# Attention scores from high and low parts instead of full float32 products, with a new instruction order

## The chip, the cores and the metric

The kernel runs on one core of a Trainium2 chip. Its time is the device time of one execution in microseconds (us). The engines are TensorE (PE: matrix products; its weight loads are shown apart, as PEld), VectorE (DVE), ScalarE (ACT), GpSimd (POOL) and SyncE (SP, which issues the transfers).

## The reference, cut to what matters

Four layers run on 8 samples of 512 rows and 256 columns. Layer 0 is causal attention with 16 heads of 16 columns, layers 1 and 3 are gated attention (only the 256 rows with the highest gate take part), layer 2 is attention with 16 heads of 64 columns and a relative bias.

```python
def _L0_attn_a_ref(x, Wq, Wk, Wv, Wo):                 # causal
    Q, K, V = (proj(Wq), proj(Wk), proj(Wv))           # 16 heads, d_k = 16
    Q = _apply_rope(Q, cos, sin)
    K = _apply_rope(K, cos, sin)
    scores = jnp.einsum('bhnd,bhmd->bhnm', Q, K) / jnp.sqrt(jnp.asarray(d_k, x.dtype))
    scores = jnp.where(causal, scores, -jnp.inf)
    attn = jax.nn.softmax(scores, axis=-1)
    ...
def _L0_ffn_ref(token_inputs, Wg, Wq, Wk, Wv, Wo):     # gated
    gate = jax.nn.sigmoid((token_inputs @ Wg)[..., 0])
    _, idx = jax.lax.top_k(gate, C)                    # C = 256 of 512 rows
    attn_in = jnp.take_along_axis(token_inputs, idx[..., None], axis=1)
    ...                                                # q, k, v: 16 heads, dh = 16
    scores = jnp.einsum('bqhd,bkhd->bhqk', q, k) / jnp.sqrt(jnp.float32(dh))
    attn = jax.nn.softmax(scores, axis=-1)
    ...
x = L0_attn_a_x                                        # (8, 512, 256)
x = x + _L0_attn_a_ref(_layernorm(x, axis=-1), ...)
x = x + _L0_ffn_ref(_layernorm(x, axis=-1), ...)
x = x + _L0_attn_b_ref(_layernorm(x, axis=-1), ...)    # 16 heads of 64, relative bias
x = x + _L0_ffn_ref(_layernorm(x, axis=-1), ...)
```

## The kernel before

All eight samples stay on the one core. The work is cut into steps such as `c_q`, `c_p1` (causal layer), `f_p1` (gated layers) and `b_row`, `b_tr`, `b_val` (biased layer). Each step is one block of TensorE work with the work of the other engines on its result. `in_order` puts all steps of all samples into one list, by the written-out numbers in `PLACE` and a model with costs per step in `WORK`; each engine goes through this list and takes its own part of each step, in that order. While sample s is in its biased layer, the causal layer and the first gated layer of sample s+1 and the last gated layer of sample s-1 are laid between its steps. So from sample 1 on the same cycle of steps repeats. Samples 0 and 1 go through their causal and first gated layers ahead of any biased step, and the last gated layer of sample 7 is alone at the end. Where the model expects TensorE to wait by over 1 us, transposes without use are put in (line 1341), which fill the wait.

TensorE writes into 8 banks of PSUM, each 128 x 512 values, and each result is read out of its bank by DVE or ACT before the bank is used again.

A score of the causal and gated layers is a product over only 16 values. Four heads are computed side by side, in four groups of 32 rows of the array, into four banks. The 32 rows of a group hold two heads; for head e of the two, `Qz` and `K1` (`Qzf`, `K1f` in gated layers) hold the head's 16 rows, zeros in the other head's, and in one of these a row of ones and the negative row maximum. The scores are computed twice:

- The first time (`c_p1`, `f_p1`, lines 1379 and 1469) rows are queries, and DVE takes the maximum of each (lines 1176 and 1251) into `mcol`.
- `c_m` and `f_m` transpose the maxima on TensorE, and DVE adds them into the row of `Qz` (line 1184).
- The second time (`c_p2`, `f_p2`, lines 1399 and 1488) rows are keys and the maximum is subtracted within the product. ACT takes the exponential straight out of PSUM (lines 1057, 1068).
- `c_va`, `c_vb`, `f_va`, `f_vb` (lines 1413, 1500) multiply the values.

A `c_p1` or `c_p2` step has a number u: its key or query tiles are 128 and 256 columns wide (u = 0 in `c_p1`, u = 2 in `c_p2`), 384 (u = 1) or 512. There are four groups g of such steps in a layer, so 12 `c_p1` and 12 `c_p2` in a causal layer, 4 `f_p1` and 4 `f_p2` in a gated one (each 2 x 256 columns). All these products are full float32.

Ahead of the scores, a causal layer turns q and k (rope): DVE shuffles and multiplies (lines 1159, 1160), POOL multiplies and adds (lines 999, 1001), then `c_hq` (ACT, lines 1051 and 1052) and `c_hk` (DVE, 1165 and 1166) make the two heads' halves. In gated layers ACT (line 1062) and DVE (line 1240) make them straight out of PSUM. Products in the reduced format `F32R` are already there in `f_gather` and `f_y` (line 1322 with `of_hi`, `of_lo`), where one factor is 0 or 1 and the other is split into a high and a low part.

```python
for t, at_, w in parts:                                    # c_p1, from line 1379's block
    for h in range(4):
        last = te.matmul(o[h][:, at_:at_ + w], m.Qz[group(h), c, e, tile_of(t)],
                         m.K1[group(h), c, e, 0:w], start=True, stop=True)
```

## Time and profile before

| | |
|---|---|
| median of 3 runs | 2102.8 us (2101.93 to 2104.2) |
| profiled execution, its own time | 2105.06 us |
| its span | 2103.3 us |
| PE busy | 2029.9 us (97%) |
| DVE, ACT, POOL busy | 1467.4, 1110.2, 600.8 us |
| the chain that ended last | PE 85%, DVE 7%, ACT 6% |

The span is the stretch from the first to the last instruction on the engines in the profiled execution; 1.8 us of its own time lie around it. Busy times are sums of instructions. A busy PE counts the pipeline of a product too, so neighbouring products overlap in it; how fast PE goes is better read from when the next ones start.

### The profile page before, as it was taken

Reading aid. Unit: us, or ns where it says so; the run is one execution under the profiler, and the core shown is the slowest. Engines: PE = TensorE matmul, PEld = TensorE weight load, DVE = VectorE, ACT = ScalarE, POOL = GpSimd, SP = SyncE. Lnnn points to the kernel's source line nnn. Section 1 sums busy time; section 2 is a strip of 40 time slices with the busy share of each in tenths; the row PEclk is TensorE's granted clock in tenths of the full one; section 3 lists DMA queues with packets and bytes.
Section 4 is the critical chain, followed back from the end, with each engine's and each line's share of the span. In section 5 each row is a group of like instructions: output and inputs, shape, how many; then the busy total and the mean of one; then the engine's idle time right before and its main releaser. Section 6 shows DMA issues by size and latency. Waiting matters only on the chain.

```text
span 2103.3 us, 38722 instructions
## 1 busy us (share of the span) xinstructions
PE 2029.9 (97%) x14644; PEld 1243.3 (59%) x14644; DVE 1467.4 (70%) x4578; ACT 1110.2 (53%) x2497; POOL 600.8 (29%) x817
## 2 busy tenths in 40 slices
PE   7889999999999999999999999999999999999997
PEld 4456556655665555765566645666456654666565
DVE  8887654777757766678767687576875777866435
ACT  1444664746537474464734646365563656535642
POOL 4212132243222342233411423124231243212220
PEclk9999999999999999999999999999999999999998
DMA  3001121121111110111101111012100121111200
GB/s 143 2 1 41 43 76 58 50 81 34 44 41 57 57 44 26 48 67 48 42 21 58 58 47 44 18 59 71 46 31 27 51 73 49 44 34 51 76 3 11
DMA packets 29047, 98.56 MB, mean 47 GB/s; under 512 B 2880, under 2 KB 11200, under 8 KB 28736
## 3 DMA queue, kind: packets, MB, share of 16 engines
q1 hardware_dynamic: 28864, 96.09, 13.6%
q8 instruction: 118, 1.93, 0.4%
q14 instruction: 65, 0.53, 0.1%
HBM read 91.89 MB, written 4.19 MB: 46 GB/s over the span
## 4 chain that ended last, share of the span: by engine, by line
PE 85%; DVE 7%; ACT 6%; issue 1%; POOL 0%; DMA 0%; SPq 0%; DVEq 0%; ACTq 0%; POOLq 0%
PE ps L861 26%; PE ps L1532 11%; PE ps L1550 10%; PE ps L1322 9%; PE ps L1540 9%; PE ps L1379 4%; PE ps L1488 3%; PE ps L1399 3%; PE ps L1500 3%; PE ps L1469 3%; PE ps L1413 2%; ACT PTc L1057 2%; ACT PT L1097 2%; DVE ps L1176 2%; DVE mcol L1251 1%; ACT probs L1088 1%
## 5 line engine op out<-in xcount | busy, mean ns | idle before, releaser
L1015 POOL TENSOR_SCALAR probs<-probs,rtotal 128x512 f32<-128x512 f32 x512 | 344.9, 693 | 871.8 <-DVE rtotal L1277 871.3
L1088 ACT ACTIVATE probs<-probs,peak 128x512 f32<-128x512 f32 x512 | 365.0, 714 | 220.9 <-DVE peak L1273 220.9
L1268 DVE CUSTOM_DVE_ANT_0 probs<-ps,band 128x512 f32<-128x512 f32 x512 | 332.6, 687 | 107.8 <-PE ps L1532 106.4
L1097 ACT ACTIVATE PT<-ps 128x512 f32<-128x512 f32 x512 | 263.1, 619 | 78.1 <-PE ps L1540 77.9
L1176 DVE CUSTOM_DVE_ANT_0 ps<-ps,later 128x128 f32<-128x128 f32 (+3 forms) x512 | 233.3, 525 | 40.9 <-PE ps L1379 40.0
L1540 PEld LDWEIGHTS ps<-ident,probs 128*128 128x128 f32 x2048 | 223.3, 141 | 52.0 <-issue 43.3
L1532 PE MATMUL ps<-KT,QT 64*128 64x512 f32 x1024 | 252.4, 611 | 0.0
L1540 PE MATMUL ps<-ident,probs 128*128 128x128 f32 x2048 | 248.3, 275 | 0.1
L1550 PE MATMUL ps<-PT,Vb 128*64 128x512 f32 x1024 | 235.9, 600 | 0.1
L861 PE MATMUL ps<-xnT,wb 128*128 128x512 f32 x512 | 233.0, 598 | 1.3 <-ACT PT L1097 0.7
L1057 ACT ACTIVATE PTc<-ps 128x384 f32<-128x384 f32 (+1 forms) x384 | 167.7, 542 | 64.8 <-PE ps L1399 64.7
L1251 DVE TENSOR_REDUCE mcol<-ps 128x2 f32<-128x512 f32 x256 | 157.3, 683 | 14.8 <-PE ps L1469 14.0
L1068 ACT ACTIVATE PTf<-ps 128x512 f32<-128x512 f32 x256 | 131.7, 604 | 63.0 <-PE ps L1488 62.6
L861 PEld LDWEIGHTS ps<-xnT,wb 128*128 128x128 f32 x512 | 92.9, 190 | 102.0 <-issue 96.8
L1532 PEld LDWEIGHTS ps<-KT,QT 64*128 64x128 f32 x1024 | 94.5, 186 | 92.9 <-issue 67.9
L1550 PEld LDWEIGHTS ps<-PT,Vb 128*64 128x64 f32 x1024 | 67.1, 137 | 139.2 <-issue 121.8
L861 PEld LDWEIGHTS ps<-wb,xnT 128*128 128x128 f32 x1024 | 122.6, 192 | 26.5 <-issue 16.7
L1007 POOL TENSOR_SCALAR_AFFINE_SELECT PTc<-PTc 128x512 f32<-128x512 f32 x128 | 82.1, 654 | 178.0 <-ACT PTc L1057 177.3
L983 POOL TENSOR_TENSOR rstd<-veps,pow_half 128x2 f32<-128x2 f32 x64 | 47.0, 737 | 280.8 <-DVE veps L1118 280.8
L861 PE MATMUL ps<-wb,xnT 128*128 128x128 f32 x1024 | 125.7, 276 | 0.0
L1322 PE MATMUL ps<-wob,OTb 128*128 128x256 f32 x512 | 114.0, 380 | 0.8 <-DVE OTb L1279 0.8
L1379 PE MATMUL ps<-K,Qz 32*128 32x128 f32 (+3 forms) x1024 | 96.5, 471 | 14.8 <-ACT PTc L1057 4.9
(133 smaller groups left out, 2887.3 us busy)
## 6 DMA issues: line engine op xcount, KB each, us to landing
band<-in_band SPq DMA_DIRECT2D x64, 896.0 KB, 4.6
wb<-in_w_b SPq DMA_DIRECT2D x64, 384.0 KB, 3.0
x<-in_x SPq DMA_DIRECT2D x16, 256.0 KB, 2.9
out<-x SPq DMA_DIRECT2D x16, 256.0 KB, 2.2
wob<-in_wo_b SPq DMA_DIRECT2D x1, 1024.0 KB, 8.7
wqk<-in_wqk_a SPq DMA_DIRECT2D x1, 512.0 KB, 6.2
cos_t<-in_cos SPq DMA_DIRECT2D x1, 256.0 KB, 5.4
sin_t<-in_sin SPq DMA_DIRECT2D x1, 256.0 KB, 6.5
```

What stands on the lines that cost most here:

```text
L861: last = nc.tensor.matmul(o, w, r, start=(i == 0), stop=(i == len(pairs) - 1))
L1015: last = g.tensor_scalar(unit, unit, rtotal[:, r % 8, e:e + 1], 1.0, ALU.mult, ALU.mult)
L1057: a.activation(pt_c(m, q)[:, h], bank(now, name)[:, 0:w], ACT.Exp).then_inc(act_read, 1)
L1088: last = a.activation(unit, unit, ACT.Exp, bias=peak[:, r % 8, e:e + 1], accum_out=total[:, r % 8, e:e + 1])
L1097: a.activation(PT[:, k % 2, e, :, tile_of(q)], bank(now, name).rearrange("p (k n) -> p k n", k=NT), ACT.Copy).then_inc(act_read, 1)
L1176: last = v.tensor_tensor_reduce(out=scores, in0=scores, in1=later[:, NT * P - w:NT * P], scale=1.0, scalar=-3e38, op0=ALU.add, op1=ALU.max ...
L1268: v.tensor_tensor_reduce(out=probs[:, r % ROWS_HELD, e, :], in0=bank(now, name), in1=band[:, k % 2, e, lo:lo + T], scale=1.0, scalar=-3e38 ...
L1322: last = te.matmul(o[:, j * D:(j + 1) * D], w, r, start=(k == 0 and j == 0), stop=(k == count - 1 and j == 1))
L1379: last = te.matmul(o[h][:, at_:at_ + w], m.Qz[group(h), c, e, tile_of(t)], m.K1[group(h), c, e, 0:w], start=True, stop=True)
L1532: full(te.matmul(bank(now, name), QT2[half(e), k % 2, tile_of(q)], KT2[half(e), k % 2, :], start=True, stop=True), now, name)
L1540: last = te.transpose(bank(now, name)[:, tile_of(t)], probs[:, r % ROWS_HELD, e, tile_of(t)], ident[:])
L1550: last = te.matmul(o[half(e), :], Vb[:, k % 3, q, half(e)], PT[:, k % 2, e, q, :], start=(q == 0), stop=(q == NT - 1))
```

## The change

The scores of causal and gated layers are computed with F32R products of split factors, in the 32 rows of a group that were half zeros before. For one head, the 16 upper rows of `X` hold the high part of q and the 16 lower ones the low part. `HI` holds the high part of k twice, `LO` its low part twice. `X` with `LO` plus `X` with `HI` is then the whole product. A `c_p1` or `f_p1` step has two F32R products in place of each float32 one. `c_p2` and `f_p2` have three: the third takes the maxima, which are now split into high and low parts as well, from a tile `M`, with a small constant of minus ones (`sel`) as weights.

To make these parts, DVE shuffles q and k twice per block (`c_dq`, `c_dk`, `f_q`, `f_k`), so that a head's 16 rows stand in both halves. For q, POOL makes both parts (`c_xq`, `f_xq`: two multiplications by a column of minus ones and zeros, two additions). For k, ACT rounds to the high part (twice) and POOL subtracts it (twice; `c_hk`, `f_hk`). The maxima are split by DVE in two small operations (`c_hm`, `f_hm`), transposed on TensorE as before, and copied out of PSUM by ACT (`c_m`, `f_m`). The factor 1/4 of the scores moves into ACT's exponential, as its scale. Tiles lie elsewhere in memory, `Dq` shares its place with `PTc`, and `M1` with `HI`, from which new rules of order follow (`lent`). The two memsets on POOL in the causal layer of sample 1 are gone; DVE does them at the start. All numbers of `PLACE` are others, found anew with the new `WORK`.

```diff
-    "c_m": [("pe", 0.443), ("dve", 1.26)],
+    "c_hm": [("dve", 0.12), ("dve", 0.16)],
+    "c_m": [("pe", 0.443), ("act", 0.5)],
...
-    "f_q": [("pe", 1.727), ("act", 1.16)],
-    "f_k": [("pe", 1.727), ("dve", 1.44)],
+    "f_q": [("pe", 1.727), ("dve", 0.65), ("dve", 0.65)],
+    "f_xq": [("pool", 0.78), ("pool", 0.78), ("pool", 1.26), ("pool", 1.26)],
+    "f_k": [("pe", 1.727), ("dve", 0.65), ("dve", 0.65)],
+    "f_hk": [("act", 0.55), ("act", 0.55), ("pool", 1.26, 0), ("pool", 1.26, 1)],
...
-    "f_p1": [("pe", 0.963), ("dve", 0.598), ("dve", 0.598), ("dve", 0.598), ("dve", 0.598)],
-    "f_m": [("pe", 0.218), ("dve", 0.74)],
-    "f_p2": [("pe", 0.972), ("act", 0.477), ("act", 0.477), ("act", 0.477), ("act", 0.477)],
+    "f_p1": [("pe", 0.47), ("dve", 0.598), ("dve", 0.598), ("dve", 0.598), ("dve", 0.598)],
+    "f_hm": [("dve", 0.12), ("dve", 0.16)],
+    "f_m": [("pe", 0.218), ("act", 0.3)],
+    "f_p2": [("pe", 0.7), ("act", 0.477), ("act", 0.477), ("act", 0.477), ("act", 0.477)],
...
-    ("c_p1", 0): [("pe", 0.85), ("dve", 0.594), ("dve", 0.594), ("dve", 0.594), ("dve", 0.594)],
-    ("c_p1", 1): [("pe", 0.858), ("dve", 0.5), ("dve", 0.5), ("dve", 0.5), ("dve", 0.5)],
-    ("c_p1", 2): [("pe", 0.965), ("dve", 0.649), ("dve", 0.649), ("dve", 0.649), ("dve", 0.649)],
-    ("c_p2", 0): [("pe", 0.975), ("act", 0.477), ("act", 0.477), ("act", 0.477), ("act", 0.477), ("pool", 0.59)],
-    ("c_p2", 1): [("pe", 0.858), ("act", 0.37), ("act", 0.37), ("act", 0.37), ("act", 0.37), ("pool", 0.59)],
-    ("c_p2", 2): [("pe", 0.863), ("act", 0.37), ("act", 0.37), ("act", 0.37), ("act", 0.37), ("pool", 1.175)],
+    ("c_p1", 0): [("pe", 0.44), ("dve", 0.594), ("dve", 0.594), ("dve", 0.594), ("dve", 0.594)],
+    ("c_p1", 1): [("pe", 0.35), ("dve", 0.5), ("dve", 0.5), ("dve", 0.5), ("dve", 0.5)],
+    ("c_p1", 2): [("pe", 0.47), ("dve", 0.649), ("dve", 0.649), ("dve", 0.649), ("dve", 0.649)],
+    ("c_p2", 0): [("pe", 0.70), ("act", 0.477), ("act", 0.477), ("act", 0.477), ("act", 0.477), ("pool", 0.59)],
+    ("c_p2", 1): [("pe", 0.53), ("act", 0.37), ("act", 0.37), ("act", 0.37), ("act", 0.37), ("pool", 0.59)],
+    ("c_p2", 2): [("pe", 0.66), ("act", 0.37), ("act", 0.37), ("act", 0.37), ("act", 0.37), ("pool", 1.175)],
...
-    "c_hq": [("act", 0.96)],
-    "c_hk": [("dve2", 0.36), ("dve2", 0.36)],
+    "c_dq": [("dve", 0.65), ("dve", 0.65)],
+    "c_xq": [("pool", 0.78), ("pool", 0.78), ("pool", 1.26), ("pool", 1.26)],
+    "c_dk": [("dve", 0.65), ("dve", 0.65)],
+    "c_hk": [("act", 0.55), ("act", 0.55), ("pool", 1.26, 0), ("pool", 1.26, 1)],
...
+        out += [(c("q", i), [c("xt")], []), (c("k", i), [c("xt")], []), (c("dq", i), [c("q", i)], []),
+                (c("xq", i), [c("dq", i)], []), (c("dk", i), [c("k", i)], []),
+                (c("hk", i), [c("dk", i)], [])]
     out += [(c("v", i), [c("xt")], []) for i in range(2)]
+    lent = {0: [c("xq", 0), c("xq", 1)], 2: [c(w, i) for w in ("q", "k", "v") for i in range(2)]}
     for g in range(4):
         for u in range(3):
-            out.append((c("p1", g, u), [c("hq", g // 2), c("hk", g // 2)], [c("p1", g, u - 1)] if u else []))
-            out.append((c("p2", g, u), [c("m", g // 2)], ([val(g - 1, u)] if g else []) + ([c("p2", g, u - 1)] if u else [])))
+            out.append((c("p1", g, u), [c("xq", g // 2), c("hk", g // 2)], [c("p1", g, u - 1)] if u else []))
+            out.append((c("p2", g, u), [c("m", g // 2)], ([val(g - 1, u)] if g else lent.get(u, [])) +
+                        ([c("p2", g, u - 1)] if u else [])))
...
-                            if kind == "c_ln" and s == 1:
-
-                                g.memset(causal[1].mcol[:], 0.0).then_inc(blank[1], 1)
-                                g.memset(causal[1].Vx[:], 1.0).then_inc(blank[1], 1)
...
+                        if kind in ("c_xq", "f_xq"):
+                            at_least(pool, w_sides, 16)
+                            if kind == "c_xq":
+                                pool.wait_ge(pairs_q_done, plan.after("pairs_q", Step("c_dq", s, l, n), now))
+                                both, parts = m.Dq[:, n], m.X[:, n]
+                            else:
+                                pool.wait_ge(dve_read, plan.unit(Step("f_q", s, l), now))
+                                both, parts = m.Dq, m.X
+                            for e in range(2):
+                                g.tensor_scalar(parts[:, e], both[:, e], sides[:, 0:1], None, ALU.mult).then_inc(signed_done, 1)
+                            for e in range(2):
+                                pool.wait_ge(signed_done, plan.after("signed", now, now) - 1 + e)
+                                last = g.tensor_tensor(parts[:, e], both[:, e], parts[:, e], ALU.add)
+                            last.then_inc(halves_q_done, 1)
+                        if kind in ("c_hk", "f_hk"):
+                            for e in range(2):
+                                pool.wait_ge(high_k_done, plan.after("high_k", now, now) - 1 + e)
+                                if kind == "c_hk":
+                                    both, high, low = m.LOf[:, n, e], m.HI[:, n, e], m.LO[:, n, e]
+                                else:
+                                    both, high, low = m.LOf[:, e], m.HI[:, e], m.LO[:, e]
+                                last = g.tensor_tensor(low, both, high, ALU.subtract)
+                            last.then_inc(halves_k_done, 1)
...
+                        if kind in ("c_m", "f_m"):
+                            parts = m.M[n][:] if kind == "c_m" else m.M[:, n]
+                            a.activation(parts, bank(now) if kind == "c_m" else bank(now)[:, 0:CAP],
                                          ACT.Copy).then_inc(act_read, 1)
-                        if kind == "c_hq":
-                            turned, other = halves(m, now)
-                            at_least(act, w_sides, 16)
-                            act.wait_ge(rope_done, plan.after("rope", Step("c_q", s, l, n), now))
-                            a.activation(other, turned, ACT.Copy, scale=sides[:, 3:4])
-                            a.activation(turned, turned, ACT.Copy, scale=sides[:, 2:3]).then_inc(halves_q_done, 1)
+                        if kind == "c_hk":
+                            act.wait_ge(pairs_k_done, plan.after("pairs_k", Step("c_dk", s, l, n), now))
+                            for e in range(2):
+                                a.activation(m.HI[:, n, e], m.LOf[:, n, e], ACT.Copy).then_inc(high_k_done, 1)
+                        if kind == "f_hk":
+                            act.wait_ge(dve_read, plan.unit(Step("f_k", s, l), now))
+                            for e in range(2):
+                                a.activation(m.HI[:, e], m.LOf[:, e], ACT.Copy).then_inc(high_k_done, 1)
...
-                    v.memset(mcol[:], 0.0).then_inc(blank[0], 1)
-                    v.memset(Vx[:], 1.0).then_inc(blank[0], 1)
+                    v.memset(peaks[:], 0.0).then_inc(blank_peaks, 1)
+                    for i in range(2):
+                        v.memset(causal[i].Vx[:], 1.0).then_inc(blank[i], 1)
...
-                            v.tensor_scalar(other, turned, sides[:, 1:2], sides[:, 5:6], ALU.mult, ALU.add)
-                            v.tensor_scalar(turned, turned, sides[:, 0:1], sides[:, 4:5], ALU.mult,
-                                            ALU.add).then_inc(halves_k_done, 1)
+                        if kind in ("c_dq", "c_dk"):
+                            turned, _ = halves(m, now)
+                            pairs, done = (m.Dq, pairs_q_done) if kind == "c_dq" else (m.LOf, pairs_k_done)
+                            dve.wait_ge(rope_done, plan.after("rope", Step("c_q" if kind == "c_dq" else "c_k", s, l, n), now))
+                            for e in range(2):
+                                last = v.stream_shuffle(pairs[:, n, e], turned, [DH * e + r % DH for r in range(32)])
+                            last.then_inc(done, 1)
+                        if kind in ("f_q", "f_k"):
+                            pairs = m.Dq if kind == "f_q" else m.LOf
+                            for e in range(2):
+                                last = v.stream_shuffle(pairs[:, e].rearrange("p c n -> p (c n)"), bank(now),
+                                                        [DH * e + r % DH for r in range(32)])
+                            last.then_inc(dve_read, 1)
...
+                        if kind in ("c_hm", "f_hm"):
+                            at_least(dve, blank_peaks, 1)
                             for e in range(2):
-                                last = v.scalar_tensor_tensor(out=rows[e], in0=peaks, scalar=sides[:, 6 + e:7 + e],
-                                                              in1=rows[e], op0=ALU.mult, op1=ALU.add)
-                            last.then_inc(dve_read, 1)
+                                dve.wait_ge(dve_read, last_unit(Step("c_p1", s, l, 2 * n + e, 2) if kind == "c_hm" else
+                                                                Step("f_p1", s, l, 2 * n + e), now))
+                            tiles = NT if kind == "c_hm" else NS
+                            top, split = peak_places(peaks, m.peaks, n, tiles), peak_places(peaks_r, m.peaks, n, tiles)
+                            v.tensor_copy(split[:, :, :, 0:2], top[:, :, :, 4:6]).then_inc(high_m_done, 1)
+                            dve.wait_ge(high_m_done, plan.after("high_m", now, now))
+                            v.tensor_tensor(split[:, :, :, 2:4], top[:, :, :, 4:6], split[:, :, :, 0:2],
+                                            ALU.subtract).then_inc(halves_m_done, 1)
...
+                                for some in (m.LO, m.HI):
+                                    for h in range(4):
+                                        last = te.matmul(o[h][:, at_:at_ + w], m.X[group(h), c, e, tile_of(t)],
+                                                         some[group(h), c, e, 0:w], start=(some is m.LO), stop=(some is m.HI))
+                                        if some is m.HI and t == parts[-1][0]:
+                                            full(last, now, names(now)[h])
...
+                                for i in range(3):
+                                    for h in range(4):
+                                        one = sel[group(h), e:e + 1].to_broadcast([32, P])
+                                        w_ = (m.LO[group(h), c, e, tile_of(t)], m.HI[group(h), c, e, tile_of(t)], one)[i]
+                                        r_ = m.M[c][group(h), t * P:T] if i == 2 else m.X[group(h), c, e, t * P:T]
+                                        last = te.matmul(o[h][:, at_:at_ + w], w_, r_, start=(i == 0), stop=(i == 2))
+                                        if i == 2 and t == parts[-1][0]:
+                                            full(last, now, names(now)[h])
```

## Rows read from the trace of the kernel before

**Rows 1.** The page of the profile, busy times of the whole span.

```profile
PE 2029.9 (97%) x14644; PEld 1243.3 (59%) x14644; DVE 1467.4 (70%) x4578; ACT 1110.2 (53%) x2497; POOL 600.8 (29%) x817
```

**Rows 2.** Busy time by stretch: start; two cycles. Then granted clock, DMA share, GB/s.

```profile
0.00:150.00 150.00, 122.40 (x1011) 69.69 (x1011) 128.51 (x412) 50.05 (x106) 48.51 (x67) 0.95 0.14 51
...
690.89:944.03 253.14, 249.09 (x1807) 151.22 (x1807) 182.35 (x572) 138.88 (x312) 74.55 (x100) 1.00 0.14 47
944.03:1197.25 253.22, 249.09 (x1807) 151.23 (x1807) 182.36 (x572) 138.90 (x312) 74.55 (x100) 1.00 0.14 47
```

**Rows 3.** PE in order of time, second scores: start, us, line, count.

```profile
765.89 1.14 PE L1399 MATMUL ps<-Qz,K 32*128 32x512 f32 x8
766.97 0.85 PE L1413 MATMUL ps<-PTc,Vx 128*32 128x384 f32 x8
767.79 0.93 PE L1399 MATMUL ps<-Qz,K 32*128 32x384 f32 x8
768.65 0.86 PE L1413 MATMUL ps<-PTc,Vx 128*32 128x256 f32 x16
769.64 0.94 PE L1399 MATMUL ps<-Qz,K 32*128 32x256 f32 x16
770.51 1.06 PE L1413 MATMUL ps<-PTc,Vx 128*32 128x512 f32 x8
...
902.21 1.15 PE L1488 MATMUL ps<-Qzf,K1f 32*128 32x256 f32 x16
903.29 1.99 PE L861 MATMUL ps<-wvf,xgT 128*128 128x256 f32 x8
```

**Rows 4.** One step of line 1469: durations in ns, first and last start.

```profile
L1469 PEld LDWEIGHTS ps<-K1f,Qzf x16: 181/185/186, 901.0 to 901.6; 32*128 32x128 f32 x16
L1469 PE MATMUL ps<-K1f,Qzf x16: 374/375/479, 901.0 to 901.8; 32*128 32x256 f32 x16
```

**Rows 5.** PE in order of time: 128-column transposes; F32R products, full array.

```profile
915.01 1.97 PE L1540 MATMUL ps<-ident,probs 128*128 128x128 f32 x16
916.81 1.99 PE L1322 MATMUL ps<-wof,OTf 128*128 128x256 f32 x8
...
924.04 0.40 PE L1322 MATMUL ps<-of_lo,spread_t 128*128 128x256 f32 x2
924.28 0.40 PE L1322 MATMUL ps<-of_hi,spread_t 128*128 128x256 f32 x2
```

**Rows 6.** Groups of DVE, ACT, POOL: busy us, mean ns of one.

```profile
L1159 DVE STREAM_SHUFFLE K<-ps 128x512 f32<-128x512 f32 x16 | 11.8, 736 | 0.0
...
L1228 DVE COPY rank<-ps 128x4 f32<-128x4 f32 x16 | 2.5, 159 | 5.6 <-PE ps L861 5.6
...
L1033 ACT ACTIVATE xn_hi<-xn 128x512 fp32r<-128x512 f32 x32 | 18.2, 614 | 0.0
...
L1015 POOL TENSOR_SCALAR probs<-probs,rtotal 128x512 f32<-128x512 f32 x512 | 344.9, 693 | 871.8 <-DVE rtotal L1277 871.3
...
L993 POOL TENSOR_TENSOR xn_lo<-xn,xn_hi 128x512 fp32r<-128x512 f32 x32 | 40.1, 1275 | 62.1 <-ACT xn_hi L1033 62.1
```

**Rows 7.** All engines in order of time, last gated layer.

```profile
2064.64 3.78 PE L861 MATMUL ps<-xgT,wkf 128*128 128x256 f32 x8 [0.69 <-ACT xgT L1059]
...
2070.40 1.26 ACT L1062 ACTIVATE Qzf<-ps,sides 128x512 f32<-128x512 f32 x2 [5.82 <-PE ps L861]
...
2071.72 2.01 PE L1469 MATMUL ps<-K1f,Qzf 32*128 32x256 f32 x32 [0.59 <-ACT Qzf L1062]
2072.88 7.27 DVE L1251 TENSOR_REDUCE mcol<-ps 128x2 f32<-128x512 f32 x12 [2.89 <-PE ps L1469]
```

**Rows 8.** All engines in order of time, start.

```profile
14.15 3.06 DVE L1125 TENSOR_SCALAR xn<-x,mv,rstd 128x256 f32<-128x256 f32 x2 [0.26 <-POOL rstd L983]
...
14.94 1.80 POOL L988 MEMSET Vx<- 128x2048 f32 x1
...
25.31 1.67 PE L1379 MATMUL ps<-K,Qz 32*128 32x128 f32 x16 [3.95 <-ACT Qz L1052]
```

612 lines of the change are left out of this document (325 added, 287 removed).

## The prediction

> **What bounds the kernel now.** I read the page first. PE is busy 97% of the span, DVE 70%, ACT 53%, POOL 29% [rows 1]. Then busy times by stretch. Two cycles of the repeating part contain the same instructions and take 253.2 us each. PE is busy 249.1 us of it, DVE 182.4, ACT 138.9 and POOL 74.6, at a granted clock of 1.00, so 2.4 GHz [rows 2]. So in a cycle TensorE is the bound: time taken from it comes off the end, until DVE's 182 us are near. The first 150 us are different: there DVE is busy 128.5 us and PE only 122.4 [rows 2], transposes without use among them. In the last gated layer the steps follow one another: PE starts the first scores at 2071.72, and DVE then reduces them for 7.27 us without a break [rows 7]. In these two stretches I credit a shorter product with nothing.
>
> **What a score step costs before.** From start to start in the order of time, a 512-column step takes 1.08 us (765.89 to 766.97), a 384-column one 0.86, a 128 + 256 one 0.87 and a gated one (two tiles of 256) 1.08 [rows 3]. A product is two instructions (a gated step has 8 products and 16 instructions, [rows 4]). 512 and 384 columns differ by 0.22 us, so 128 columns of a float32 product cost 0.215, and 256 cost 0.43. Of a 512-column step 0.86 us are then streaming, and 0.22 us are fixed: the first weights loaded ahead of the first product, the array run empty behind the last. The same 0.22 closes the others: 0.86 = 0.64 + 0.22, 0.87 = 0.65 + 0.22, and 1.08 = 4 x 0.215 + 0.22 for the gated step. Four heads run side by side: 16 instructions of 0.375 us start within 0.8 us [rows 4].
>
> **What one costs after.** No F32R product in a 32-row group is in the trace. The nearest row is F32R on the whole array: two products of 256 columns in 0.24 us (924.04 to 924.28), 0.12 each [rows 5]. float32 streams 256 columns in 0.43, so F32R takes a quarter, 0.107, and a little over it. That little is the weight load: 16 transposes of 128 columns take 1.80 us, 0.1125 each, although 128 columns stream in half of it [rows 5]. So a round of four heads can't be shorter than about 0.12. I take 0.12 for 128 and 256 columns, 0.16 for 384 and 0.215 for 512 (the quarter of float32), and leave the fixed 0.22, which comes from entering and leaving the 32-row groups and of which nothing is changed. Ends for a round of 128 columns: 0.055 (streaming alone) and 0.215 (as float32).
>
> - First scores, two rounds per tile: 128 + 256 columns 4 x 0.12 + 0.22 = 0.70 (saves 0.17); 384 columns 0.54 (0.32); 512 columns 0.65 (0.43). Together 0.92.
> - Second scores, three rounds: 512 columns 3 x 0.215 + 0.22 = 0.865 (saves 0.215); 384 columns 0.70 (0.16); 256 + 128 columns 6 x 0.12 + 0.22 = 0.94, which is 0.07 more than before. Together 0.305.
> - Four groups: 4 x 1.225 = 4.9 us per causal layer.
> - Gated: `f_p1` 4 x 0.12 + 0.22 = 0.70 (saves 0.38), `f_p2` 6 x 0.12 + 0.22 = 0.94 (0.14). Four of each: 2.1 us per layer.
>
> A cycle has one causal and two gated layers, so 9.1 us. Of the eight causal layers, samples 2 to 7 lie in the part bound by PE; of the sixteen gated ones all but the first layers of samples 0 and 1 and the very last. That is 6 x 4.9 + 13 x 2.1 = 56.7 us.
>
> A rule of the Trainium skill speaks against this: TensorE: Matmul & The Clock Gate, Part 3 on packing small matmuls, says that a weight load overlaps with running matmuls only when it goes to another row group. Here every round uses all four groups, so by it each load would be exposed. The trace speaks against the rule for float32: the 16 loads of a step start from 901.0 to 901.6, while its products run [rows 4]. What exposed loads would give is the rival below.
>
> **The other engines.** In a cycle DVE gets 8 + 8 shuffles of 0.736 and four pairs plus four pairs at most of small operations, an estimate of 0.4 us a pair: 15 us, even if nothing were taken from it (it loses `c_hk`, line 1240 and line 1184). ACT gets 8 roundings of 0.614 and six copies not longer than that, 8.6 us, and loses some. POOL gets four blocks of queries (2 x 0.693 + 2 x 1.275 = 3.94) and four of keys (2.55), 26 us [rows 6]. That gives at most DVE 197, ACT 147, POOL 101 in a cycle of 244 us: none of them becomes the bound, and in sum I cost them at nothing. The cover is the biased layer's TensorE work between these steps. If it is gone, a block costs up to its whole 3.94 us; queued behind it on POOL are `b_nrm`, for which `b_tr` waits, and `c_p2`'s masking. The Trainium skill's TensorEngine Tiling (Array Packing), PSUM Bottleneck, warns that emptying PSUM may become the bound once products are packed; the engines that empty it stay under 81% here by the rows, so it would change the sum by nothing.
>
> The rules of order by shared memory (`lent`) and the copy of the maxima by ACT only bind steps within a layer; a cycle has others to put between. Costed at zero, with 1 us a block kept for a rival.
>
> **Start.** Before, the first scores begin at 25.31, after waiting 3.95 us for ACT [rows 8]. After, two shuffles (1.47), the key's two subtractions (2.55) and the query's four POOL operations (3.94) stand there in place of ACT's two (1.4): +6.5. POOL's memsets are gone; DVE's normalisations, begun at 14.15, ended 0.5 us behind the second of them, at 17.2 [rows 8]. Without it I let them end 2.2 us earlier, an estimate. Then DVE is the bound, with about the same work. Net +4 us, between 0 and 10.
>
> **End.** The first product after the gather starts at 2064.64, the query's is done near 2070.2, ACT takes 1.26 and the scores begin at 2071.72 [rows 7]. With the query first: its product takes what the key's took, to 2068.2 (3.78 us less the overlap), shuffles to 2069.7, POOL to 2073.7, the key's subtractions to 2076.2. So +4.5; the rest is bound by DVE's maxima and ACT's exponentials, which stay. I take +5, between 2 and 8.
>
> **Sum.** -56.7 + 4 + 5 = -48 us. The profiled execution took 2105.1, so 2057; the median of the runs is 2.3 lower than that execution: 2055 us.
>
> **The rivals.**
>
> - *The new POOL blocks cost a little* (19%). A cycle has four query blocks; PE stands 1 us at each, four times in some 6.5 cycles, 26 us: 2081. For it: TensorE follows a fixed order and has only 4.1 us without work in a cycle [rows 2], so any late part is seen. Against: POOL is idle 70% of the time.
> - *They cost all of it, and the kernel is slower* (7%). PE stands 3.94 us at each: 15.8 a cycle against the 9.1 gained, +43 in all, with start and end 2155. It decides from 2.3 us per block.
> - *Exposed loads* (5%). Each round is 0.107 longer than its stream. Second scores of 256 + 128 columns then take 1.35 us, `f_p2` 6 x 0.215 + 0.22 = 1.51; per causal layer +2.0, per gated one +1.7, in all +34, with start and end 2146. The start times in [rows 4] speak against it.
> - *The fixed part shrinks or the order has it less often* (15%). The kernel's own new costs in `WORK` have 0.35 for 384 columns and 0.47 for a gated first step: streams with a tenth on top. By them a causal layer saves 8.9 and a gated one 3.1, in all 93 us: 2019. For it: two such steps in a row could share entry and exit. Against: the steps of before show 0.22 at every width, and nothing in it depends on the format.
> - *The forecast* has 54%. Its own range is 2036 to 2074: 11 us more if 128 columns go at float32's speed (5 rounds x 0.095 x 4 x 6), 8 less if only by streaming, 5 to either side for start and end, and up to 10 less if the new order removes some of the 4.1 us of waits per cycle.
>
> The range for 8 in 10 takes the two middle rivals' near sides: 2016 to 2092. Within 0.2% (4 us) counts as no change, about what a measurement of this kernel can tell. Faster 0.87 (forecast, small cost, smaller fixed part, less a hundredth), same 0.02, slower 0.11 (the two slow rivals, less what falls between).
>
> **What the new profile would show.** Right: rounds of four F32R products 0.12 us apart at 256 columns; `f_p1` steps of 0.70 and `f_p2` of 0.94 from start to start; a cycle near 244 us with PE still over 97% busy; POOL near 100 us of it; first scores near 29 us and, in the last layer, some 12 us after the gather's copy. Wrong: rounds of 0.2 us or more at 256 columns (loads exposed); PE waits released by POOL's `X` or `LO` that sum to over 25 us; a cycle under 240 us (fixed part shrunk).

## The result, and the profile after

The changed kernel takes **2141.2 us** (median of 4 runs, 2139.0 to 2144.4) against 2103.4 for the kernel before: ratio 1.018, interval 1.0165 to 1.0198. It is slower; 2055 was forecast, with 2016 to 2092 as the range. Where the 34.4 us by which the span grew (2103.3 to 2137.7) lie can be read off by the samples' last `b_y`, the output products of the biased layer (the start of the last of its instructions). The first comes at 361.5 us, before 351.8 (+9.7). Six cycles take 258.1, 259.3, 255.6, 255.7, 260.2 and 254.7 us, before 253.1 or 253.2 each (+24.5). The seventh stretch, the last biased layer, takes 170.1 instead of 175.6 (-5.5), and what is behind it 62.6 instead of 56.9 (+5.7).

The same windows as in [rows 2], of the kernel after: two cycles and the first 150 us.

```profile
0.00:150.00 150.00, 112.50 (x973) 73.79 (x977) 122.92 (x433) 42.28 (x88) 80.90 (x87) 0.83 0.14 51
1116.31:1371.97 255.66, 241.06 (x1941) 151.58 (x1940) 187.10 (x596) 139.71 (x318) 106.42 (x124) 1.00 0.14 46
1371.97:1632.17 260.20, 246.38 (x1941) 155.79 (x1940) 187.02 (x596) 140.17 (x318) 106.39 (x124) 0.97 0.14 46
```

In the first of the two cycles TensorE is busy 241.1 us, 8.0 less than before: the work did get shorter, nearly by the 9.1 foreseen. But TensorE stands 14.6 us in that cycle (before 4.1), and in the second the granted clock falls to 0.97 as well. POOL is busy 106.4, the start's clock is 0.83 (before 0.95). What TensorE waits for, over the whole span, total, times and longest in us:

```profile
PE ps L1477 <- DVE peaks L1274: 23.6, 26, 2.1
PE ps L1572 <- DVE peaks L1348: 17.9, 13, 2.2
PE ps L926 <- DVE above L1323: 13.4, 8, 2.8
PE ps L1572 <- issue: 13.1, 6, 2.2
PE ps L1572 <- POOL gX L1075: 11.0, 7, 1.7
...
PE ps L1477 <- POOL X L1075: 3.6, 1, 3.6
PE ps L1572 <- POOL gLO L1084: 3.6, 1, 3.6
```

L1477 and L1572 are the first scores of a causal and a gated layer. Their waits are for DVE's maxima, which empty the banks, and for POOL's operands `X`, `gX`, `gLO` and `LO` (18.4 us in all, with one of 0.2 that is not shown). "issue" is waiting for which the profile names no other engine.

A gated first-score step and the instruction behind it, PE in order of time; then a second-score step of 512 columns (they answer to [rows 3]):

```profile
1174.09 0.39 PE L1572 MATMUL ps<-gLO,gX 32*128 32x256 f32 x4 [0.41 <-DVE peaks L1348]
1174.29 0.31 PE L1572 MATMUL ps<-gHI,gX 32*128 32x256 f32 x4
1174.40 0.32 PE L1572 MATMUL ps<-gLO,gX 32*128 32x256 f32 x4
1174.52 0.31 PE L1572 MATMUL ps<-gHI,gX 32*128 32x256 f32 x4
1174.77 0.49 PE L926 MATMUL ps<-wb,xnT 128*128 128x128 f32 x2
...
1265.69 0.50 PE L1501 MATMUL ps<-X,LO 32*128 32x512 f32 x4
1266.02 0.40 PE L1501 MATMUL ps<-X,HI 32*128 32x512 f32 x4
1266.26 0.40 PE L1501 MATMUL ps<-M,sel 32*128 32x512 f32 x4
```

Behind the first round of 256 columns (0.20 to the next) the rounds start 0.11 to 0.12 us apart, and the step takes 0.68 from start to start; a round of 512 columns takes 0.24 (1266.02 to 1266.26), behind the first (0.33). So the terms for TensorE held. The groups of POOL (busy us, mean ns of one, idle before) show one that did not; [rows 6] had 693 ns for the nearest instruction:

```profile
L1099 POOL TENSOR_SCALAR probs<-probs,rtotal 128x512 f32<-128x512 f32 x512 | 345.1, 694 | 540.9 <-DVE rtotal L1374 540.1
...
L1072 POOL TENSOR_SCALAR gX<-gDq,sides 128x512 fp32r<-128x512 f32 x32 | 49.9, 1567 | 25.5 <-DVE gDq L1264 25.5
L1072 POOL TENSOR_SCALAR X<-Dq,sides 128x512 fp32r<-128x512 f32 x32 | 49.7, 1564 | 0.0
```

The multiplication by `sides` takes 1.57 us where `b_nrm`'s takes 0.69. Both are TENSOR_SCALAR on 128x512 float32 from SBUF with a scale per partition. They differ in the output's type and in the code: `b_nrm` gives two operations (`scale, 1.0, mult, mult`), the new line one (`scale, None, mult`). In the last gated layer the whole chain lies open (all engines in order of time, answering to [rows 7]):

```profile
2096.94 3.11 POOL L1072 TENSOR_SCALAR gX<-gDq,sides 128x512 fp32r<-128x512 f32 x2 [13.05 <-DVE gDq L1264]
...
2100.02 2.49 POOL L1075 TENSOR_TENSOR gX<-gDq,gX 128x512 fp32r<-128x512 f32 x2
...
2102.47 2.48 POOL L1084 TENSOR_TENSOR gLO<-gLOf,gHI 128x512 fp32r<-128x512 f32 x2
2105.09 0.39 PE L1572 MATMUL ps<-gLO,gX 32*128 32x256 f32 x4 [3.58 <-POOL gLO L1084]
```

A query block is 5.6 us instead of 3.94, and the first scores start behind it and the key's subtractions.

### The profile page after: what moved, and what is told of

The parts are those of the page before. It is cut to its first block, busy times and chain, and to the rows that moved or that the text cites. A ratio compares the mean times of both kernels' runs of the same rounds, so it can differ in the third digit from the quotient of the medians.

```text
span 2137.7 us, 41526 instructions
## 1 busy us (share of the span) xinstructions
PE 1987.2 (93%) x15737; PEld 1266.5 (59%) x15737; DVE 1499.3 (70%) x4771; ACT 1121.0 (52%) x2546; POOL 853.3 (40%) x1007
## 4 chain that ended last, share of the span: by engine, by line
PE 71%; DVE 15%; ACT 6%; POOL 4%; issue 2%; DVEq 0%
PE ps L926 21%; PE ps L1639 10%; PE ps L1419 9%; PE ps L1647 8%; PE ps L1657 8%; DVE peaks L1348 4%; DVE ps L1274 3%; PE ps L1501 3%; PE ps L1515 3%; PE ps L1606 2%; PE ps L1594 2%; DVE probs L1365 2%; ACT PTf L1160 2%; PE ps L1477 2%; ACT PTc L1153 2%
## 5 line engine op out<-in xcount | busy, mean ns | idle before, releaser
L1274 DVE CUSTOM_DVE_ANT_0 ps<-ps,later 128x512 f32<-128x512 f32 (+3 forms) x512 | 232.8, 524 | 33.3 <-PE ps L1477 32.9
L1639 PE MATMUL ps<-KT,QT 64*128 64x512 f32 x1024 | 244.7, 607 | 0.0
L1348 DVE TENSOR_REDUCE peaks<-ps 128x2 f32<-128x512 f32 x256 | 157.0, 682 | 64.7 <-PE ps L1572 64.7
L1419 PEld LDWEIGHTS ps<-wob,OTb 128*128 128x128 f32 x512 | 96.4, 190 | 12.6
```

Of the source, the lines that this page charges most:

```text
L1274: last = v.tensor_tensor_reduce(out=scores, in0=scores, in1=later[:, NT * P - w:NT * P], scale=1.0, scalar=-3e38, op0=ALU.add, op1=ALU.max ...
L1348: v.tensor_reduce(places[:, h:h + 1].rearrange("p h t -> p (h t)"), bank(now, name).rearrange("p (t n) -> p t n", t=NS), AXIS.X, ALU.max). ...
L1419: last = te.matmul(o[:, j * D:(j + 1) * D], w, r, start=(k == 0 and j == 0), stop=(k == count - 1 and j == 1))
L1639: full(te.matmul(bank(now, name), QT2[half(e), k % 2, tile_of(q)], KT2[half(e), k % 2, :], start=True, stop=True), now, name)
```

## The experiments

The "cycle" below is from one sample's last `b_y` to the next; "first" is the time of the first one. Both are read from the profiled execution, which is one of the 4 to 10 that the time is the median of. The edits are changes to the kernel after, if nothing else is said, and are shown cut to what matters. TensorE's time without work in a cycle is its length less PE's busy time.

**The form of POOL's multiplication.**

```diff
-g.tensor_scalar(parts[:, e], both[:, e], sides[:, 0:1], None, ALU.mult)
+g.tensor_scalar(parts[:, e], both[:, e], sides[:, 0:1], 1.0, ALU.mult, ALU.mult)
```

> POOL's multiplication for the query's parts is written with two operations (times the column of sides, times 1.0), the form of b_nrm's, which takes 0.69 us; the new one has one operation and takes 1.56. Same result. Theory A (the multiplications are 0.87 us longer each than the order was laid out for, and the scores wait for them): the instruction falls to about 0.7 us if its form is the cause, POOL's busy time falls by some 55 us, a cycle from 255.6 to near 250, the whole by 25 to 40 us (2100 to 2115). If the reduced output format is the cause instead, nothing moves. Theory B (the new order itself leaves TensorE idle, whatever the multiplications take): under 10 us less even if the instruction falls.

2107.6 us (ratio to before 1.0019, 1.0007 to 1.0031), cycle 252.6, first 362.1. The 32 instructions, durations in ns (min/median/max):

```profile
L1072 POOL TENSOR_SCALAR X<-Dq,sides x32: 682/697/720, 28.5 to 1746.3; 128x512 fp32r<-128x512 f32 x32
```

One added operation by 1.0 makes the instruction 0.87 us shorter and the kernel 34 us. The output's type is the same in both, so it is the form. TensorE's waits for POOL's operands fall from 18.4 us to 4.9, and the 13.1 put down to "issue" are gone, so they hung on POOL too. That loss is explained. 52 us to the forecast are left, nearly all that the products should have brought.

**The multiplications on ScalarE.** ScalarE makes them with the scale per partition, in its queue at the same place of the order; POOL only adds.

> ACT makes the two multiplications of the query's parts (with its scale), POOL only the two additions; same result, same order of steps. A query block leaves POOL 3.1 us shorter and costs ACT 1.25 us. Theory A: like the two-operation form or a little better, 25 to 45 us less than the changed kernel (2096 to 2115), since each half is ready about 1.8 us earlier; also DVE's small operations that went from 0.195 to 0.269 us go back. Theory B: under 10 us less. If ACT's queue is what matters, slower than the changed kernel.

2173.7 us (1.033). Two waits of PE, as above:

```profile
PE ps L1580 <- POOL gX L1073: 26.9, 6, 4.5
PE ps L1485 <- POOL X L1073: 24.4, 7, 4.0
```

ScalarE in order of time in one gated layer:

```profile
1366.27 5.99 ACT L1197 ACTIVATE PT<-ps 128x512 f32<-128x512 f32 x12 [2.02 <-PE ps L1655]
1372.02 1.43 ACT L1136 ACTIVATE gX<-gDq,sides 128x512 fp32r<-128x512 f32 x2
```

DVE's second shuffle of this `gDq` ends at 1364.5. POOL is relieved and its result comes later all the same: the chain now passes through the queue of an engine that has other work ordered ahead, here twelve copies of `PT`. What counts is when the result is ready, not how long POOL is busy.

**The products alone.** The kernel before, with its order and all its other work; only the score products are replaced by two (first scores) or three (second scores) rounds of F32R from a constant tile, so the scores are not the reference's.

```diff
-last = te.matmul(o[h][:, at_:at_ + w], m.Qz[group(h), c, e, tile_of(t)], m.K1[group(h), c, e, 0:w], ...)
+for i in range(2):
+    for h in range(4):
+        last = rounds(o[h][:, at_:at_ + w], h, w, 2, i)   # lhs and rhs: dummy, 128x128 F32R
```

> The kernel before, with its order and all work of the other engines, in which only TensorE's score products are replaced: two rounds of F32R products in the first scores, three in the second, all from a small constant tile (the scores are not the reference's). It is the TensorE part of the change alone. By the prediction's sum: 4.9 us less per causal and 2.1 per gated layer in the part bound by TensorE, so a cycle near 244 and the whole near 2046 (2036 to 2055), since start and end have no longer chain. If the gain in TensorE time can't be had in this kernel at all because DVE and ACT empty the banks too slowly (theory C), a cycle stays over 250 and the whole over 2085.

2072.6 us (0.985, 0.9836 to 0.9868), cycle 248.3, first 350.6. PE is busy 240.9 us of a cycle, as in the kernel after, and stands 7.3 (before 4.1): of the 8 us less work 4.8 arrive. That lies between the two expectations. Then the same kernel with the places of the steps searched anew by the kernel's own planner, first as it is, then with one more wait on POOL (see the meeting at `f_row` below):

> The kernel before with the score products alone replaced by rounds over a constant tile (as in the run of the products alone: 2072.6, cycle 248.3; the scores are not the reference's), and now the places of the steps searched anew with the measured costs of the score steps: the planner's cycle falls from 247.4 to 244.2 us, its total from 2040 to 2013. Theory A: the half of the products' saving that did not come was held back by the order, which was made for the longer products: cycle 244.5 to 246, time 2042 to 2056. Rival B: the banks' emptying takes it whatever the order: cycle 247.5 to 248.5, time 2065 to 2075.

> The kernel before with the score products alone replaced by rounds over a constant tile and the places searched anew for them, and with POOL's wait of the run before: f_part's two subtractions begin only when the same layer's comparisons (tie, above) are done. Without that wait its cycle was 247.5 to 249.0 us where the planner has 244.2, with one wait of TensorE for above of 2.5 us per cycle; the new places put f_part right behind f_row, where the kernel before has it seven steps ahead. Theory A: the order can pay the other half of the products' saving, and the meeting of DVE and POOL took it back: cycle 245 to 246.5, time 2048 to 2057. Rival B: with the meeting gone the wait goes to the next bank, cycle 247.3 or more, time above 2062.

2067.2 us (0.982, 0.9806 to 0.9839; cycles 247.5 to 249.0), where the rival had it, and with the wait **2051.4** (0.9755, 0.9741 to 0.977; cycle 246.6). The row of that cycle:

```profile
1088.30:1335.00 246.70, 240.22 (x1936) 151.19 (x1935) 180.27 (x572) 138.50 (x312) 74.42 (x100) 1.00 0.15 48
```

The control is the kernel before itself, with searched places and that wait:

> The kernel before with nothing changed but the places of its steps, searched anew for half an hour with its own costs (the planner's total falls from 2076 to 2060, its cycle from 252.2 to 250.6 us), and POOL's wait at f_part; the result is the same. It is the control for the products alone with searched places (2051.4 us, cycle 246.6). Theory A: most of those 52 us are the products': TensorE is busy 249.1 of 253.1 us here, so little is to be had, cycle 251.5 to 253.2, time 2092 to 2104. Rival B: the search itself is worth a third or more of it: cycle 250.5 to 251.4, time below 2088.

2104.9 us (0.9999, 0.999 to 1.0009), cycle 254.4, longer than either theory had and than the planner's 250.6. The search and the wait alone give nothing in sum, so the 52 us are the shorter products', and they come in full only in an order made for them: 31 in the old order, 52 in their own (one search each). The sum hides two parts: the control's cycles are 1.3 us longer than before, and its seventh stretch is 169.4 us instead of 175.6. The products' own order has that shorter stretch too (168.3), which is 6.1 of the 17.6 us that it gains over the old order by the profiled executions; 10.1 lie in the six cycles.

**The clock in the start.** With the two-operation form; ahead of each causal first-score step of the first two samples:

```diff
+if kind == "c_p1" and s < 2 and l == 0:
+    room(now, names(now)[0])
+    for i in range(4):
+        te.transpose(bank(now, names(now)[0])[:, tile_of(i % NT)], ident[:], ident[:])
```

> The kernel after with POOL's multiplication in its two-operation form, and ahead of each first-score step of the causal layers of the first two sequences four 128x128 transposes that compute nothing (24 steps, 0.14 us each at full clock, 13 us in all); the result is the same. In the kernel with the two-operation form TensorE was granted 0.67 of full speed from 50 to 100 us, and the first repeated b_y ends at 362.1 us; the kernel before had 1.00 there and 351.8. Theory A: the low clock is a price of its own, caused by TensorE's pauses for DVE's maxima (11.3 us in eight waits): with the pauses partly filled the granted clock of 50 to 100 us rises above 0.85 and the first b_y comes at 356 to 361 us although 13 us of work are added; time 2102 to 2106. Rival B: the clock is only a sign of the pauses and costs nothing, because DVE bounds the start: b_y comes later by up to the 13 us added, 365 to 375, time 2111 to 2120.

2101.7 us (0.9994, 0.9984 to 1.0003), first 352.1, cycle 252.6. The first `b_y` comes 10 us earlier with 13 us more work, in the fastest of this kernel's ten executions; by the medians the whole is 5.9 us shorter. The windows from 50 to 60 and 60 to 70 us of the kernel before, then of the one with the two-operation form (the eighth number is the granted clock):

```profile
50.00:60.00 10.00, 6.85 (x68) 3.07 (x64) 10.00 (x43) 4.66 (x11) 5.09 (x5) 1.00 0.00 1
60.00:70.00 10.00, 8.88 (x104) 3.93 (x104) 8.57 (x27) 6.94 (x17) 3.59 (x6) 1.00 0.01 2
```

```profile
50.00:60.00 10.00, 6.84 (x60) 4.40 (x60) 9.12 (x36) 6.23 (x14) 3.21 (x4) 0.50 0.01 2
60.00:70.00 10.00, 6.90 (x60) 3.35 (x60) 7.66 (x34) 1.92 (x5) 5.50 (x7) 0.50 0.00 0
```

Before, the clock is 2.4 GHz here, now 1.2, with the same busy time in the first of the two windows. From 30 to 110 us TensorE had stood 1.9 us for `X`, with 32.37 as its end, and then 11.3 us in eight waits for DVE's maxima, four of them before 50. With the transposes the clock of 50 to 100 us is 0.86 instead of 0.67.

**The meeting at `f_row`.** The kernel just measured, and POOL begins `f_part`'s two subtractions only when the same layer's comparisons are done:

```diff
 if kind == "f_part":
+    at_least(pool, above_done, plan.after("above", Step("f_row", s, l), now))
```

> The kernel with the two-operation form and the transposes in the start, and one wait more: POOL begins the two subtractions of f_part (xn_lo) only when the comparisons of the same layer's f_row (tie, above) are done; the result is the same. In the repeating cycle two of the four tie instructions of one gated layer take 1.36 us instead of 0.35, each beside one of these subtractions (1.27 us), and behind them TensorE waits 1.3 us for above and the next first scores come 2.3 us later than the kernel's planner has them. Theory A: this meeting of DVE and POOL is part of what is left in the cycle: all ties at 0.35 us, the wait for above gone, cycle from 252.6 to 251.0 or 251.5, time 2091 to 2097 (from 2101.7). Rival B: the chain only waits for xn_lo instead (it is done 2.6 us after above), cycle 252.3 to 253, time 2099 to 2105.

**2093.3 us** (0.9945, 0.993 to 0.996), cycle 251.4, first 353.2: faster than both kernels, with the reference's result. The profiled executions differ by only 3.0 us (5.6 less in the six cycles, 1.1 more ahead of the first `b_y`, 1.5 more at the end), since the one compared with is the fastest of its ten and this one the slowest of its four. All engines in order of time, first without the wait (two-operation form), then with it:

```profile
1308.01 3.18 DVE L1319 SCALAR_TENSOR_TENSOR tie<-gate_row,gate,before 128x128 bf16<-128x128 f32 x4
...
1308.33 2.71 POOL L1054 TENSOR_TENSOR xn_lo<-xn,xn_hi 128x512 fp32r<-128x512 f32 x2 [5.48 <-ACT xn_hi L1117]
...
1312.69 0.47 DVE L1323 TENSOR_SCALAR above<-gate_row,gate 128x512 bf16<-128x512 f32 x1
...
1313.22 0.18 PE L926 MATMUL ps<-ones,tie 128*128 128x1 bf16 x1 [1.32 <-DVE above L1323]
```

```profile
1295.69 1.14 DVE L1320 SCALAR_TENSOR_TENSOR tie<-gate_row,gate,before 128x128 bf16<-128x128 f32 x4
...
1298.32 0.48 DVE L1324 TENSOR_SCALAR above<-gate_row,gate 128x512 bf16<-128x512 f32 x1
...
1298.88 1.28 POOL L1055 TENSOR_TENSOR xn_lo<-xn,xn_hi 128x512 fp32r<-128x512 f32 x1 [8.37 <-DVE above L1324]
```

Four `tie` instructions take 3.18 us beside POOL's subtractions and 1.14 without them; the two long ones take 1.36 and 1.37. The kernel before has `f_part` seven steps ahead of `f_row` in each cycle; the new order has it right behind, so this meeting came with the change (before, `tie` reaches 1.4 us only in the start and in the last layer). So did another in the order that was searched for the products.

**Another order.** That kernel's steps placed anew, with the planner's costs of the score steps and of the parts set to the measured ones; without and with POOL's wait:

> The kernel with the two-operation form and the transposes in the start, with the planner's costs of the score steps and of the parts' steps set to what the trace of the kernel after showed, and the places of the steps searched anew with them (half an hour; the planner's own total falls only from 2052 to 2046, its cycle stays at 248.3 us); the result is the same. Theory A: the order given is near the best of its kind, and what is left is in the chains: cycle 250 to 252.6, time 2086 to 2100. Rival B: the order is what holds the gain back: cycle 248.5 or below and time below 2080.

> The kernel with the two-operation form, the transposes in the start and the places searched anew, with POOL's wait at f_part added (as it took the given order from 252.6 to 251.4 us); the result is the same. Without it its cycle was 252.3 to 255.3 us. Theory A: what is left lies in the chains, not in the order: cycle 250.8 to 251.6, time 2089 to 2097, no better than the given order with that wait (2093.3). Rival B: with the meeting gone the searched order shows its worth: cycle at or below 249.5, time below 2085.

2103.6 us (0.9992, 0.9979 to 1.0005; cycles 252.3 to 255.3) and 2091.5 (0.9947, 0.9931 to 0.9964; cycle mostly 252.6, first 349.7). The given order was as good as what the search found, and the searched one was slower than its theory had. As the control shows, the planner's cycle and the measured one differ by more than such a search moves them, so this says little of orders farther off. The forecast's rival of 2019, a smaller fixed part, is answered by the steps themselves: 0.68 us for `f_p1`, not 0.47.

**The loads.** From the two-operation form, either POOL leaves out the two additions of each query block (its parts are then not the reference's), or DVE's maxima read half the columns of each tile (and the exponential's scale is 0.01; the maxima are not the reference's):

```diff
-    last = g.tensor_tensor(parts[:, e], both[:, e], parts[:, e], ALU.add)
```

```diff
-scores = bank(now, name)[:, o:o + w]
+scores = bank(now, name)[:, o:o + w // 2]      # mask and gated maxima likewise
```

> The kernel after with the two-operation form, and of POOL's query block only the two multiplications are made, the two additions (1.27 us each) left out everywhere, so that the block takes 1.4 instead of 3.9 us; the query's parts are thereby not the reference's. Theory A: with the two-operation form the block is no longer what the cycle waits for; what is left of the loss is the emptying of the banks by DVE and ScalarE: the cycle stays between 251.5 and 252.6 us (252.6 with the whole block), the time between 2099 and 2106, most of it from the start. Rival B: POOL's 16 additions per cycle (10 us less of it) still stand in TensorE's way: cycle 248 to 250, time 2080 to 2092.

> The kernel after with the two-operation form, and DVE's maximum over the first scores (causal and gated layers) reads only half of each tile's columns; with it the scale of the exponential is 0.01, so that nothing overflows. The scores' maxima and everything behind them are thereby not the reference's. TensorE, POOL and ScalarE do the same work. Theory A: TensorE's rounds are now shorter than the time in which DVE empties four banks, so the first-score steps run at DVE's rate: with 48 maxima of the causal and 32 of the gated layers per cycle each some 0.2 us shorter TensorE's waits for the maxima (42 us in all) fall below 15 us, the cycle goes from 252.6 to between 246 and 249.5 us and the time to between 2060 and 2085. Rival B: the waits for the maxima come from the order (DVE busy elsewhere when the scores come) and stay: cycle above 251, time above 2095.

2104.4 us (1.0, 0.9989 to 1.001; cycle mostly 252.6, first 356.9) and 2086.4 (0.992, 0.9902 to 0.9935; cycle 251.0, first 349.6). POOL's part was as good as nothing in the cycles and 3.2 us in all. DVE's was half a refutation of my theory: 18.7 us less DVE work per cycle gave 1.6 us, and the wait at `above` stayed. Over half of what it gave lies in the start, where the first `b_y` comes 12.5 us earlier. With POOL's wait and the transposes in place, both loads together and then each alone:

> The version so far best (two-operation form, transposes in the start, POOL's wait at f_part: 2093.3 us, cycle 251.4) with two loads lifted at once: DVE's maxima read half of each tile's columns (with 0.01 as the exponential's scale) and POOL leaves out the two additions of each query block. The scores are thereby not the reference's. DVE falls to some 167 us of a cycle, below the 182 of the kernel before; POOL to some 89. With the products alone and searched places the cycle was 246.6. Theory A: it is not the load of the two engines that holds the cycle above 246.6 but how long the chain from a query's product to its scores and maxima is, and the places where the order makes TensorE meet it; the cycle stays between 249 and 250.5, time 2072 to 2083. Rival B: the load it is; with it gone the cycle falls to 247.5 or less and the time below 2062.

> The version with POOL's wait at f_part (2093.3 us, cycle 251.4, first b_y 353), and POOL leaves out the two additions of each query block (2.5 us of 3.9); the query's parts are thereby not the reference's. Theory A: POOL's part of the new chain is off the path here too, as it was without the wait: cycle 251.0 to 251.6, time 2086 to 2094, at most the start gains. Rival B: with the meeting at f_row gone, the block is what the scores wait for: cycle 249.5 or less, time below 2078.

> The version with POOL's wait at f_part (2093.3 us, cycle 251.4, first b_y 353), and DVE's maxima read half of each tile's columns, with 0.01 as the exponential's scale; the maxima are thereby not the reference's. Theory A: DVE's emptying of the banks is what holds the cycle, and it alone accounts for the 3.0 us per cycle and most of the 17 us of the start that both loads together gave: cycle 248.4 to 249.0, first b_y at 337 to 342, time 2053 to 2062. Rival B: each load hides the other, so that one alone gives little, as without the wait: cycle 249.8 to 250.4, time 2070 to 2080.

2053.0 us (0.976, 0.974 to 0.978; cycle 248.4, first 336.3), 2087.1 (0.992, 0.9906 to 0.9936; cycle mostly 250.4, first 348.2) and 2066.8 (0.983, 0.9811 to 0.9844; cycle 249.4, first 340.4). None of the first pair of theories was met (cycle 248.4, where one had 249 or more and the other 247.5 or less); for the single loads it came out between as well: DVE's maxima are two thirds of it (26.5 of 40.2 us), POOL's additions 6 to 14, by what else is lifted. What TensorE waits for DVE's maxima ahead of first scores in one cycle, with whole and with halved maxima:

```profile
PE ps L1577 <- DVE peaks L1349: 2.5, 2, 1.4
PE ps L1482 <- DVE peaks L1275: 2.1, 3, 1.1
```

```profile
PE ps L1483 <- DVE peaks L1276: 0.9, 1, 0.9
PE ps L1578 <- DVE peaks L1350: 0.6, 1, 0.6
```

The maxima are work of the kernel before as well, and that kernel was not run with halved ones. So these runs show that TensorE waits for them, not how much of that is new. The row of the cycle with both lifted:

```profile
1081.60:1330.00 248.40, 240.24 (x1941) 151.66 (x1940) 166.15 (x596) 139.34 (x318) 89.32 (x116) 1.00 0.15 48
```

## Why the prediction was wrong

**The step that failed first** is "POOL gets four blocks of queries (2 x 0.693 + 2 x 1.275 = 3.94)". Its 0.693 came from an instruction with two operations; the new one has one and takes 1.565. A block is 5.67 us, and the term decided the sign: the one-word edit is worth 34 us and brings the kernel to 0.2% above the one before. Of the 86 us between forecast and result it explains 34. The rival "cost all of it, decides from 2.3 us per block" had the right engine and the right side, at 7%, but by a mechanism in which only whether TensorE waits was open, not what the block takes. I had held the row to be the same instruction, and gave that term no second end. The sign that I had named for it came in part: waits for POOL's `X` or `LO` of 18.4 us, and 31.5 with those under "issue", against 25.

**The second**, with the other 52 us, is "in sum I cost them at nothing" of the other engines. It compared busy times (they came out inside my bounds: DVE 187, ACT 140, POOL 99.6 with the two-operation form) and asked whether one becomes the bound. None did. But TensorE runs a fixed order on eight banks, and it meets the others at points, not in sums. The products alone, with the old order, brought 31 of the 52 us that they are worth: in a cycle TensorE's listed waits grew from 3.2 us to 6.7, those for DVE from 1.6 to 4.1 and those for ScalarE from 1.6 to 2.3. In the changed kernel, halving DVE's maxima is worth 26.5 us although DVE is busy under 75% of a cycle. By the profiled executions, which are 30.0 us apart, 12.8 lie ahead of the first `b_y`, where I had DVE as the bound already, and 13.2 in the six cycles, where I had put nothing.

The Trainium skill's TensorEngine Tiling (Array Packing), PSUM Bottleneck, says that emptying PSUM may become the bottleneck once TensorE is faster; I said that it would change the sum by nothing. The trace agrees with the page so far as the waits for the maxima go, 4.6 us in a cycle and 1.5 with halved ones, though no engine that empties the banks is busy all the time.

**The third** is the start: +4 foreseen, +9.7 measured. The first scores begin at 34.56, not near 29. The normalisations did end 2.4 us earlier (14.75), as let; but the chain behind them took 5.2 us more than my +6.5. The long multiplications are 1.7 of that. The rest is POOL's queue (all engines in order of time):

```profile
20.18 1.15 ACT L1139 ACTIVATE HI<-LOf 128x512 fp32r<-128x512 f32 x2 [3.73 <-DVE LOf L1259]
...
21.29 1.28 POOL L1060 TENSOR_TENSOR HIf<-HIf,sin_t 128x512 f32<-128x512 f32 x1
...
25.22 1.28 POOL L1062 TENSOR_TENSOR Xf<-Xf 128x512 f32<-128x512 f32 x1
...
26.46 2.51 POOL L1084 TENSOR_TENSOR LO<-LOf,HI 128x512 fp32r<-128x512 f32 x2
...
34.56 0.33 PE L1477 MATMUL ps<-LO,X 32*128 32x128 f32 x4 [3.62 <-POOL X L1075]
```

The key's high parts are ready at 21.33, but four rotations of the other half of query and key, 1.28 us each and the first begun at 21.29, stand ahead of the subtractions, which begin at 26.46. And I took the end of that chain for the whole price. With the two-operation form the first `b_y` is no earlier (362.1). What cost the time were the pauses, for `X` and for DVE's maxima, and that TensorE behind them ran at 1.2 GHz for parts of the next 100 us; filling some of them brought the first `b_y` forward by 10 us in the profiled execution, and the whole by 5.9 in the medians.

**The fourth** was named nowhere: the new order puts POOL's subtractions beside DVE's comparisons. It costs 1.2 us per cycle, and 8.4 in all by the medians. This and the start's pauses are parts of the 52 us.

**What held.** TensorE's terms: rounds of 0.12 at 256 columns and 0.24 at 512 (0.215), `f_p1` 0.68 (0.70), `f_p2` 0.91 (0.94), 8.0 of the 9.1 us less work in a cycle. Weight loads are hidden although every round uses all four row groups: by my estimate for the rival with exposed loads a round of 256 columns would have taken 0.21. The sentence of the Trainium skill's TensorE: Matmul & The Clock Gate, Part 3, that a load overlaps with running products only when it goes to another row group, does not hold in this trace: the loads of the second round start at 1174.17, while the first round's products, on the same groups, run for 0.39 us from 1174.09. The end, +5.7 for +5, by luck in part: the block was 1.7 us too short there and the rest too long.

**What stays open.** From 2093.3 to 2051.4 us. Lifting half of DVE's maxima and POOL's additions gives 2053.0, but not in the same places. Of the 41.1 us by the profiled executions, 29.6 lie in the six cycles (251.4 against 246.6), and the lifted loads bring 19.5 of those; the rest of what they bring is mostly in the start (16.9), where the products alone are only 4.6 us ahead. So load is part of it, and 10 us of the cycles are left without a cause. How much is the new work itself (DVE's shuffles, POOL's blocks) and how much the place of the maxima in the order, the runs don't separate. That the search found nothing for the changed kernel and 21 us for the products alone (with the wait) says only that near its order there is nothing that this planner sees.

All versions beside one another (us; ratio to before):

| version | time | ratio | cycle | first `b_y` |
|---|---|---|---|---|
| before | 2103.4 | 1 | 253.1 | 351.8 |
| after | 2141.2 | 1.018 | 254.7 to 260.2 | 361.5 |
| + two-operation form | 2107.6 | 1.002 | 252.6 | 362.1 |
| + transposes in the start | 2101.7 | 0.999 | 252.6 | 352.1 |
| + POOL's wait at `f_part` | 2093.3 | 0.9945 | 251.4 | 353.2 |
| + DVE's maxima halved | 2066.8 | 0.983 | 249.4 | 340.4 |
| + POOL's additions left out | 2053.0 | 0.976 | 248.4 | 336.3 |
| before, searched order and wait | 2104.9 | 1.000 | 254.4 | 351.5 |
| before, products alone | 2072.6 | 0.985 | 248.3 | 350.6 |
| products alone, searched order and wait | 2051.4 | 0.9755 | 246.6 | 348.6 |

## What to carry to other kernels

Take a duration only from a row whose instruction is the same down to its operands; where the row differs in one argument, give the term a second end and price it. Where the bounding engine follows a fixed order and shares banks with the others, a shorter instruction on it can be worth less than it takes off the busy time, by what the emptying of its banks and the order allow: put the new work in with the old operands replaced by a constant and measure that alone before building the rest. And when an order is made anew, look at which instructions on DVE and POOL now stand side by side.

## What the runs showed of the hardware

- POOL's TENSOR_SCALAR on 128x512 float32 from SBUF with a scale per partition: 1.57 us with one operation, 0.70 with two, the second a multiplication by 1.0.
- DVE's SCALAR_TENSOR_TENSOR on 128x128 with a bf16 operand takes 0.35 us alone and 1.36 to 1.37 beside one of POOL's TENSOR_TENSOR on 128x512 float32 (1.43 and 1.33 us there, 1.28 alone). DVE's gated reductions from PSUM take 0.67 to 0.69 us throughout the same execution.
- TensorE at 1.2 GHz is as busy as at 2.4 in such windows (6.84 and 6.85 us of 10): the busy share hides it, the granted clock shows it.
- ScalarE with its scale per partition gave the same result as POOL's multiplication in 0.72 to 0.75 us in the mean, about as short as POOL's two-operation form, and the kernel took 66 us more than with that form: the operands came later from its queue.
